# Expert tiles of the second half: results scattered to token order instead of gathered, with new order tables

## The chip, the cores and the metric

One core of one Trainium2 chip runs the kernel. The metric is the device time in microseconds (us) of one execution.

## What is computed

The input is x, 4 batches of 256 tokens of 128 numbers. Four layers are added to it one after the other, each on a layernormed x:

```
x = x + cross_attention_0(ln(x), ctx)       # 8 heads of 64, 512 context rows of 96
x = x + ffn_0(ln(x))                        # 128 -> 512 -> 128, fixed point, piecewise-linear gelu
x = x + cross_attention_1(ln(x), ctx)       # 16 heads of 8, then its own 128 -> 256 -> 128
x = x + moe(ln(x))                          # 8 experts, each token goes to its best two
# moe, per token t: sum over its two experts e of share[t, e] * (silu(t @ W1[e]) * (t @ W3[e])) @ W2[e]
```

## The kernel before

**One order for all engines.** `schedule()` makes one list of some 740 steps. A step is a name with indices, such as `("max", 1, 3, 5)`. Each engine walks the same list and executes its own part of each step, so the list sets the order of work within each of the five queues (PE, DVE, ACT, POOL, SP) and semaphores tie them together. The place of a step comes from tables: `PLACES` (per layer) and `SHIFTED` (per batch of a layer) give a place counted in attention heads, a pair meaning first place and distance. `REST` does this for the last part, in expert tiles.

**Attention** (places in heads): for each head, `max` computes scores and their row maxima on DVE (L879), `rows` transposes four heads' maxima on PE and copies them below the queries (L893), `sc` computes scores (L606) with an exponential on ACT (L1190), `av` multiplies with the values (L625, L638). Between them stand the steps of the feed-forward layer, of projections, loads of expert weights (`stage`) and their split in two fp16 parts on POOL (`split`).

**The mixture of experts** runs in two halves of 512 tokens (NT = 4 token tiles of 128, batches 0-1 and 2-3). For each half:
- `logits`, `route`, `shares`, `compare`, `rank` and `best` find the two best experts and their shares, all small DVE instructions. `rank` gives a mask, `count` counts tokens per expert on PE, and `place` (L1055 and on) gives each token two slots in a table of SLOTS = 15 tiles of 128 rows, sorted by expert, each expert's rows starting a new tile. `weights` puts the shares in the order of the two slots.
- `send` (POOL, L1360): eight indirect DMAs write 128 rows of 512 B each to the table `slots_in` in DRAM. `fetch` (SP, L1507) loads the table in four pieces, `gT` (L507, L1260, L1095) transposes and splits them.
- For each tile k (0 to 14 for half 0, 15 to 29 for half 1): `gu` (gate and up matmuls L781, silu L1268, product L1101), `hT` (transposes L792, L1274, L1105) and `dn` (down matmuls L800 and L803, ACT copy L1280, DVE sum L1112 into `y_sb`, four buffers, `k % 4`). `gu` of tile k has place k, `hT` k + 1.3, `dn` k + 2.6. SP's part of `dn` is `keep` (L1511): it stores the 64 KB result to the DRAM table `slots_out`, and DVE's next use of the buffer waits for that.
- `pick` (POOL, L1372): when all 15 stores of a half have landed, eight indirect DMAs gather the rows that belong to each token tile. `mix` (DVE, L1118 and L1119) adds two weighted rows to x, `store` (SP, L1515) writes the token tile out.

`pick 0` and `mix 0` run under tiles of half 1; `route`, `shares`, `best` and `weights` of half 1 stand behind tile 29, and `pick 1` and `mix 1` come last. In the profile names, `probs` holds y_sb and the gathered rows, `kS` and `kx` hold tokens and small arrays of this part, since buffers are used again.

Of the kernel before, what the change touches and what calls it, by code (L numbers as in the profile page):

```python
# [34 lines left out]
GROUPS = -(-SLOTS // 4)  # L35

# [3 lines left out]
    0: {"max": (1.86, 0.79), "sum": -0.41, "av": (3.3, 0.77), "f_ln": -2.84, "f_xn": -2.17, "f_xT": 4.05,  # L40
        "up0": (1.6, 0.1), "round": 7.85, "floor": 1.73, "nodes": -2.0, "slope": 6.04, "interp": 1.03,
# [3 lines left out]
        "zeros": -0.77, "wipe": -3.06, "init": (1.9, 2.63), "stack": 2.57, "rows": 3.42},  # L45
    1: {"max": (1.92, 0.8), "av": (1.04, 0.72), "f_ln": 1.67, "f_xn": 10.53, "f_xT": -6.55, "up0": (1.44, 0.53),
        "round": 2.56, "floor": 4.44, "nodes": 0.43, "slope": -4.29, "interp": 5.35, "ident": 12.62, "down0": 2.09,
        "q1_ln": 3.44, "q1_xn": 17.99, "q1_xT": 1.73, "q1": 12.78, "k1": 10.57, "bounce": 17.73, "sT": 2.58,
        "oT": (-3.52, 2.41), "aT": (3.56, 1.1), "y0": (3.34, 2.45), "oT1": (14.23, 0.44), "aT1": 4.66, "h1": 7.81,
        "y1": 15.69, "v1": 3.6, "stack": -2.4, "stage": (3.94, 1.45), "split": (1.35, 2.26), "consts": -5.47,  # L50
        "ex_ln": (4.78, 1.56), "ex_xn": (7.31, 1.05), "ex_xT": (5.75, 0.75), "logits": (9.25, 1.44),
        "route": 12.16, "shares": 10.26, "compare": 21.8, "rank": 21.45, "best": 18.11, "count": 18.16,
        "place": 17.23, "weights": 15.2, "send": 25.91, "fetch": 14.23, "gT": (19.54, 0.64), "rows": 3.88},
# [4 lines left out]
    (0, 'aT'): (3.66, 0.59), (0, 'av'): (-0.24, 0.54), (0, 'bounce'): 2.36, (0, 'down0'): 1.14, (0, 'f_ln'): -2.7,  # L58
    (0, 'f_xT'): 2.05, (0, 'f_xn'): 3.77, (0, 'floor'): -0.49, (0, 'ident'): 5.31, (0, 'init'): (1.06, 1.93),
    (0, 'interp'): 2.18, (0, 'k0'): (5.1, 0.6), (0, 'k1'): 2.26, (0, 'max'): (3.93, 0.56), (0, 'nodes'): 2.37,  # L60
    (0, 'oT'): (8.2, 1.03), (0, 'q0'): (6.54, 1.04), (0, 'q0_ln'): -1.54, (0, 'q0_xT'): 3.93, (0, 'q0_xn'): 2.69,
    (0, 'q1'): 4.85, (0, 'q1_ln'): 2.47, (0, 'q1_xT'): 8.92, (0, 'q1_xn'): 1.31, (0, 'round'): 3.34,
# [9 lines left out]
    (1, 'v0'): (7.68, 0.92), (1, 'v1'): 7.35, (1, 'wipe'): -3.17, (1, 'y0'): (6.57, 0.93), (1, 'zeros'): 6.25,
    (2, 'aT'): (5.59, 1.32), (2, 'av'): (-0.03, 0.96), (2, 'bounce'): 5.4, (2, 'down0'): 4.02, (2, 'f_ln'): -1.27,
    (2, 'f_xT'): 1.24, (2, 'f_xn'): 0.67, (2, 'floor'): 1.94, (2, 'ident'): 3.41, (2, 'init'): (-1.87, 2.14),
    (2, 'interp'): 3.32, (2, 'k0'): (2.17, 0.05), (2, 'k1'): 2.04, (2, 'max'): (1.54, 1.0), (2, 'nodes'): 2.29,
    (2, 'oT'): (5.07, 0.82), (2, 'q0'): (1.15, 1.29), (2, 'q0_ln'): -4.48, (2, 'q0_xT'): 1.23, (2, 'q0_xn'): -0.71,
    (2, 'q1'): 5.61, (2, 'q1_ln'): 4.16, (2, 'q1_xT'): 5.38, (2, 'q1_xn'): 4.63, (2, 'round'): 1.71,
    (2, 'rows'): 0.77, (2, 'sT'): 3.91, (2, 'slope'): 2.96, (2, 'stack'): 2.21, (2, 'sum'): 2.31,
    (2, 'up0'): (1.52, 0.14), (2, 'v0'): (3.77, 1.09), (2, 'v1'): 3.48, (2, 'wipe'): -0.07,
    (2, 'y0'): (6.04, 1.73), (2, 'zeros'): 8.64, (3, 'aT'): (5.76, 1.46), (3, 'av'): (-0.45, 0.96),  # L80
    (3, 'bounce'): 6.0, (3, 'down0'): 4.15, (3, 'f_ln'): -5.52, (3, 'f_xT'): 1.37, (3, 'f_xn'): 0.93,
    (3, 'floor'): 1.82, (3, 'ident'): 3.77, (3, 'init'): (-1.89, 2.22), (3, 'interp'): 3.51,
# [3 lines left out]
    (3, 'sT'): 3.7, (3, 'slope'): 3.25, (3, 'stack'): -6.1, (3, 'sum'): 1.34, (3, 'up0'): (1.58, 0.12),  # L86
    (3, 'v0'): (2.92, 0.59), (3, 'v1'): 5.21, (3, 'wipe'): 1.45, (3, 'y0'): (7.01, 0.57), (3, 'zeros'): 2.35,
    (4, 'aT'): (6.57, 2.0), (4, 'aT1'): 11.18, (4, 'av'): (-0.04, 1.0), (4, 'best'): 13.86, (4, 'bounce'): 12.33,
    (4, 'compare'): 14.92, (4, 'consts'): 12.05, (4, 'count'): 10.96, (4, 'down0'): 7.65,
    (4, 'ex_ln'): (9.16, 1.4), (4, 'ex_xT'): (9.35, 0.76), (4, 'ex_xn'): (8.67, 1.04), (4, 'f_ln'): 1.16,  # L90
# [1483 lines left out]
```

## Time and profile before

| | |
|---|---|
| median of 3 runs | 451.77 us (451.18 to 452.14) |
| the profiled execution's own time | 449.94 us |
| its span, first to last instruction | 447.8 us |
| mean granted TensorE clock | 0.941 |
| busy: PE / DVE / ACT / POOL | 381.1 / 323.1 / 241.6 / 195.3 us |
| HBM read / written | 15.11 / 7.86 MB |

Busy time is the time in which an engine executes; the rest of the span it waits. A row of the timeline gives the start, the busy time, the engine, the line of the kernel, the operation and output <- input; in brackets stands the idle time ahead of it and what ended it. The durations below are of the one profiled execution.

### The profile page before, as it was taken

What the parts mean: (1) busy time and instruction counts of PE and PEld (TensorE: products, weight loads), DVE (VectorE), ACT (ScalarE), POOL (GpSimd) and SP (SyncE); (2) the same over time, 40 slices, a digit from 0 to 9 for tenths busy, and PEclk for the clock granted to TensorE, in tenths of its full rate; (3) what the DMA queues carried; (4) which work ended last, traced back from release to release, by engine and by line L of the source; (5) the groups of instructions that cost most, each with busy time, mean ns of one, the idle gap of its engine ahead of it and who ended that gap; (6) DMA issues with size and microseconds to landing.
All of it is one profiled execution on the core that took longest, in us unless ns stands there. A gap on an engine that the chain in (4) does not pass through costs nothing.

```text
span 447.8 us, 8284 instructions
## 1 busy us (share of the span) xinstructions
PE 381.1 (85%) x2778; PEld 220.3 (49%) x2778; DVE 323.1 (72%) x668; ACT 241.6 (54%) x473; POOL 195.3 (44%) x252
## 2 busy tenths in 40 slices
PE   8667789999779868996997899998999789999930
PEld 3414444665356445553544355553454456777620
DVE  5765594667785799779888998789851685677752
ACT  3614455655734552467476666764676444665530
POOL 5135987726464493744418134660540015015014
PEclk9957999999899989998999699998999999999985
DMA  6572708008106106422043105420030002412112
GB/s 184 129 195 53 173 1 196 16 16 197 37 1 192 58 0 151 109 72 71 25 133 91 48 5 153 113 74 2 31 108 1 6 24 62 124 37 67 40 38 64
DMA packets 44766, 34.67 MB, mean 77 GB/s; under 512 B 5965, under 2 KB 41229, under 8 KB 44429
## 3 DMA queue, kind: packets, MB, share of 16 engines
q1 hardware_dynamic: 43701, 32.03, 27.6%
q0 software_dynamic: 1024, 2.10, 1.6%
q8 instruction: 24, 0.39, 0.4%
q14 instruction: 17, 0.14, 0.1%
HBM read 15.11 MB, written 7.86 MB: 51 GB/s over the span
## 4 chain that ended last, share of the span: by engine, by line
PE 51%; DVE 18%; issue 9%; ACT 8%; DMA 6%; POOL 4%; SPq 4%; POOLq 0%; DVEq 0%; ACTq 0%
PE p_sc L606 7%; PE p_misc L576 5%; PE p_o L625 5%; DVE mx L879 4%; PE p_misc L507 4%; PE p_misc L781 4%; PE p_sc L781 4%; PE p_o L638 4%; SPq L1434 4%; PE p_o L792 3%; PE p_misc L800 3%; PE p_misc L533 2%; DMA slots_in<-qx,kx 2%; DVE xn L849 2%; ACT probs L1190 2%
## 5 line engine op out<-in xcount | busy, mean ns | idle before, releaser
L879 DVE TENSOR_REDUCE mx<-p_misc 128x1 f32<-128x512 f32 x192 | 122.4, 683 | 26.3 <-PE p_misc L576 25.2
L1190 ACT ACTIVATE probs<-p_sc 128x512 f32<-128x512 f32 x192 | 104.5, 597 | 57.0 <-PE p_sc L606 56.4
L576 PE MATMUL p_misc<-kS,qS 96*128 96x512 f16 x128 | 40.9, 393 | 6.4 <-DVE mx L879 6.3
L606 PE MATMUL p_sc<-qS,kS 128*128 128x256 f16 x256 | 42.1, 283 | 3.2 <-ACT probs L1190 2.6
L1304 POOL TENSOR_SCALAR veps<-meanvar 128x2 f32<-128x2 f32 x16 | 3.8, 235 | 90.9 <-DVE meanvar L835 90.5
L1346 POOL TENSOR_TENSOR psums<-probs 128x256 f32<-128x256 f32 x32 | 24.7, 773 | 42.1 <-PE p_o L632 39.2
L638 PE MATMUL p_o<-probs,v 128*32 128x256 f32 x512 | 41.3, 401 | 0.4 <-issue 0.3
L625 PE MATMUL p_o<-probs,v 128*64 128x256 f32 x256 | 35.1, 395 | 4.0 <-ACT probs L1190 3.9
L1101 DVE TENSOR_TENSOR probs<-probs,p_sc 128x512 f32<-128x512 f32 x30 | 20.6, 686 | 24.4 <-ACT probs L1268 24.1
L1372 POOL DMA_INDIRECT probs<-slots_out,kx x16 | 15.2, 948 | 50.4 <-DMA slots_out<-probs 40.1
L606 PE MATMUL p_sc<-region 128*128 128x256 f16 x256 | 35.8, 286 | 0.9 <-DVE region L893 0.9
L1268 ACT ACTIVATE probs<-p_misc 128x512 f32<-128x512 f32 x30 | 17.9, 597 | 32.3 <-PE p_sc L781 32.3
L606 PEld LDWEIGHTS p_sc<-qS,kS 128*128 128x128 f16 x256 | 21.5, 100 | 25.9 <-issue 10.3
L606 PEld LDWEIGHTS p_sc<-region 128*128 128x128 f16 x256 | 24.8, 102 | 13.4 <-issue 5.2
L1360 POOL DMA_INDIRECT slots_in<-qx,kx x16 | 15.7, 984 | 33.3 <-issue 27.1
L1394 POOL TENSOR_TENSOR region<-v,region 128x512 f16<-128x512 f32 x24 | 28.8, 1200 | 1.9
L576 PE MATMUL p_misc<-region 128*128 128x512 f16 x64 | 21.8, 414 | 7.6 <-DVE cT L863 3.1
L1347 POOL TENSOR_TENSOR psums<-psums,probs 128x256 f32<-128x256 f32 x32 | 26.3, 821 | 2.5
L1348 POOL TENSOR_TENSOR psums<-psums,probs 128x256 f32<-128x256 f32 x32 | 25.5, 796 | 2.5
L625 PEld LDWEIGHTS p_o<-probs,v 128*64 128x64 f32 x256 | 15.8, 136 | 19.1 <-issue 9.4
L1393 POOL CAST region<-v 128x512 f16<-128x512 f32 x24 | 16.7, 695 | 15.8 <-DMA v<-in_L_ffn_W_dram 14.8
L1105 DVE TENSOR_TENSOR probs<-p_o,probs 128x512 f16<-128x512 f32 x30 | 20.5, 685 | 2.5 <-ACT probs L1274 2.5
(206 smaller groups left out, 741.5 us busy)
## 6 DMA issues: line engine op xcount, KB each, us to landing
region<-kx SPq DMA_DIRECT2D x24, 256.0 KB, 3.9
v<-in_L_ffn_W_dram SPq DMA_DIRECT2D x24, 256.0 KB, 2.8
region<-qx SPq DMA_DIRECT2D x24, 128.0 KB, 3.9
slots_in<-qS SPq DMA_DIRECT2D x2, 960.0 KB, 7.0
slots_out<-probs SPq DMA_DIRECT2D x30, 64.0 KB, 1.5
kS<-kS SPq DMA_DIRECT2D x1, 1664.0 KB
kS<-k_scratch SPq DMA_DIRECT2D x8, 192.0 KB
kS<-slots_in SPq DMA_DIRECT2D x6, 256.0 KB, 3.4
```

The source lines that it names most:

```text
L576: pe.matmul(ps, q[:, i * P:(i + 1) * P], k, start=True, stop=True).then_inc(full, 1)
L606: last = pe.matmul(p_sc[:, half, j * S:(j + 1) * S], k[:, kt * P:(kt + 1) * P], q, start=(i == 0), stop=(i == len(pairs) - 1))
L625: pe.matmul(p_o[64 * i:64 * i + 64, 0, m * S:(m + 1) * S], v0[:, b % 2, kt, h * DH0:(h + 1) * DH0], probs[:, h % 8, kt * S:(kt + 1) * S], ...
L638: last = pe.matmul(p_o[32 * j:32 * j + 32, n % 2, 0:S], v1[:, b % 2, c, h * VW:h * VW + 32], probs[:, h % 8, c * S:(c + 1) * S], start=(c ...
L781: last = pe.matmul(ps[:, k % 2, :], takenT[half][:, xs, at], w[:, bass.ds(chosen[k], 1), ws, :].rearrange("p e n -> p (e n)"), start=(i == ...
L879: dve.tensor_reduce(mx[:, b % 2, i, h:h + 1], ps, AX_X, ALU.max).then_inc(free, 1)
L1101: dve.tensor_tensor(hp[:, k % 2, :], sg[:, k % 2, :], p_sc[:, k % 2, :], ALU.mult).then_inc(hp_done, 1)
L1190: act.activation(probs[:, h % 8, half * 512:(half + 1) * 512], p_sc[:, half, :], ACT.Exp, scale=(DH0 if layer == 0 else DH1) ** -0.5).then ...
L1346: link(pool.tensor_tensor(psums[:, h % 4, :], tiles[0], tiles[1], ALU.add))
L1347: link(pool.tensor_tensor(psums[:, h % 4, :], psums[:, h % 4, :], tiles[2], ALU.add))
L1348: pool.tensor_tensor(psums[:, h % 4, :], psums[:, h % 4, :], tiles[3], ALU.add).then_inc(sums_set, 1)
L1394: pool.tensor_tensor(low, whole, high, ALU.subtract).then_inc(stage_free, 1)
```

## The change

In words: half 1's tile results no longer go to a slot table that is gathered once it is complete. Each row is scattered, as soon as its tile is done, to a DRAM table `token_rows` in which a token's two rows stand side by side, and SP then loads this table with plain DMAs.

- A row must know its destination. So the rows of half 1 get two more numbers (WIDE = 130, 520 B): twice the token's number plus 2, and the slot of the token's first row. They are written by DVE in `numbers` (new; one small matmul on PE and five DVE instructions, behind `aT1 3`) and in `place`, travel through send and fetch, and `dest` (new, four DVE instructions, between `dn 12` and `gu 15`) makes 15 columns of row numbers of them. Rows without a token get a row of their own at the table's end.
- `dn` of tiles 15 to 29 has a part on POOL, `to_tokens`, an indirect DMA, and none on SP. DVE waits for `y_sent` instead of `y_kept`.
- `pick` now has one step per token tile of half 0, each with two gathers, spread between tiles: pick 0 ahead of `hT 16` (so ahead of `dn 15`), pick 1 behind `dn 16`, pick 2 ahead of `dn 19`, pick 3 ahead of `dn 22`. Pick 1 of half 1 is gone; `back` (SP) waits for the last four scatters and loads four pieces of 128 KB, and `mix 1` waits for these.
- The four tables are rewritten. Of the mixture's steps: `best 0` and `weights 0` go from around `place 0` to the last batch (heads 1 and 12), `count 0` gets one max and one av step ahead of it, half 0's `gT` goes from head 11 and 12 to 14 and 15, `split 23` goes ahead of `send 0`, `fetch 1` from behind `dn 6` to behind `dn 8` (SP queue), and half 1's four late routing steps stay behind `dn 29`. In the attention parts most steps move by a few places; POOL's queue changes in 5 neighbouring exchanges there, SP's in 2.

```diff
-        (3.63, 'compare', 1), (3.68, 'rank', 1), (31.7, 'route', 1), (31.71, 'shares', 1), (31.72, 'best', 1), (31.73, 'weights', 1),
-        (4.79, 'count', 1), (4.84, 'place', 1), (5.44, 'send', 1), (8.85, 'fetch', 1), (13.62, 'gT', 1, 0),
-        (15.75, 'gT', 1, 1), (17.72, 'gT', 1, 2), (18.76, 'gT', 1, 3), (19.42, 'pick', 0), (20.61, 'mix', 0, 0),
-        (21.99, 'mix', 0, 1), (26.65, 'mix', 0, 2), (31.47, 'mix', 0, 3)]
+REST = [(0.16, 'oT1', 3, 0), (0.76, 'oT1', 3, 1), (1.09, 'aT1', 3), (1.16, 'numbers'), (1.77, 'h1', 3),
+        (1.82, 'y1', 3), (1.9, 'ln', 'ex', 3), (2.98, 'xn', 'ex', 3), (3.45, 'xT', 'ex', 3), (3.48, 'logits', 3),
+        (3.5, 'compare', 1), (3.92, 'rank', 1), (4.74, 'count', 1), (4.95, 'place', 1), (9.2, 'send', 1),
+        (11.34, 'fetch', 1), (13.99, 'gT', 1, 0), (14.99, 'dest'), (15.89, 'gT', 1, 1), (17.15, 'pick', 0),
+        (18.05, 'gT', 1, 2), (18.87, 'pick', 1), (20.69, 'gT', 1, 3), (21.4, 'pick', 2), (23.92, 'mix', 0, 0),
+        (24.54, 'pick', 3), (24.74, 'mix', 0, 1), (26.49, 'mix', 0, 2), (27.66, 'mix', 0, 3), (36.2, 'route', 1),
+        (38.8, 'shares', 1), (45.58, 'best', 1), (49.06, 'weights', 1)]
...
-    order += [("pick", 1)] + [("mix", 1, i) for i in range(NT)]
+    order += [("back",)] + [("mix", 1, i) for i in range(NT)]
...
+            def numbers():
+                pe.wait_ge(consts_set, 1)
+                ps, full = misc_take(pe, ("numbers",))
+                pe.matmul(ps[:, 0:SLOTS], before[:, :], all_ones[:, 0:SLOTS], start=True, stop=True).then_inc(full, 1)
...
+                if half == 1:
+                    dve.tensor_scalar(rows1[:, :, P + 1], slot[:, 0, :], 1.0, None, ALU.subtract)
...
+            def numbers():
+                dve.wait_ge(consts_set, 1)
+                ps, free = misc_wait(dve, ("numbers",))
+                link(dve.scalar_tensor_tensor(rows1[:, :, P], turn[:, 0:NT], float(P), ps[:, 0:NT], ALU.mult, ALU.add))
+                dve.tensor_scalar(rows1[:, :, P], rows1[:, :, P], 2.0, 2.0, ALU.mult, ALU.add)
+                dve.scalar_tensor_tensor(slot_number[:, :], turn[:, :], float(P), ps[:, 0:SLOTS], ALU.mult, ALU.add).then_inc(free, 1)
+                misc_done(dve, ("numbers",))
+                link(dve.tensor_scalar(own_row[:, :], slot_number[:, :], 2.0 * NT * P + 2, None, ALU.add))
+            def destinations():
+                for q in range(GROUPS):
+                    dve.wait_ge(ld_taken[q], 16 * 2)
+                link(dve.tensor_tensor(is_first[:, :], taken[:, :, P + 1], slot_number[:, :], ALU.is_equal))
+                link(dve.scalar_tensor_tensor(own_row[:, :], taken[:, :, P], 0.0, own_row[:, :], ALU.is_equal, ALU.mult))
+                link(dve.tensor_tensor(own_row[:, :], own_row[:, :], is_first[:, :], ALU.add))
+                dve.tensor_tensor(dest[:, :], taken[:, :, P], own_row[:, :], ALU.add).then_inc(dest_set, 1)
...
             def result(k):
-                if k >= 4:
+                if 4 <= k < SLOTS + 4:
                     dve.wait_ge(y_kept[k % 4], 16 * (k // 4))
+                elif k >= 4:
+                    dve.wait_ge(y_sent[k % 4], 16 * sent_of(k - 4))
...
+            def pick(i):
+                for s in range(4):
+                    pool.wait_ge(y_kept[s], 16 * ((SLOTS + 3 - s) // 4))
+                if i:
+                    pool.wait_ge(picked[i - 1], 16 * 2)
+                for s in range(2):
+                    pool.indirect_dma_start(picks[0][:, s, i, :], None, d_out,
+                                            bass.IndirectOffsetOnAxis(ap=slot_id[:, 0, s, i:i + 1], axis=0)).then_inc(picked[i], 16)
+            def to_tokens(k):
+                if k < SLOTS:
+                    return
+                misc_done(pool, ("ym", k))
+                if k == SLOTS:
+                    pool.wait_ge(dest_set, 1)
+                pool.indirect_dma_start(d_rows, bass.IndirectOffsetOnAxis(ap=dest[:, k - SLOTS:k - SLOTS + 1], axis=0),
+                                        y_sb[:, k % 4, :], None).then_inc(y_sent[k % 4], 16)
...
+            def back():
+                for k in range(2 * SLOTS - 4, 2 * SLOTS):
+                    sp.wait_ge(y_sent[k % 4], 16 * sent_of(k))
+                for i in range(NT):
+                    sp.dma_start(picks[1][:, :, i, :], d_rows[2 + 2 * P * i:2 + 2 * P * (i + 1), :].rearrange("(p s) n -> p s n", s=2)).then_inc(y_back[i], 16)
```

## Rows read from the trace of the kernel before

**Rows 1.** The page's busy time of each engine.
```profile
PE 381.1 (85%) x2778; PEld 220.3 (49%) x2778; DVE 323.1 (72%) x668; ACT 241.6 (54%) x473; POOL 195.3 (44%) x252
```

**Rows 2.** By stretch: length, busy PE, PEld, DVE, ACT, POOL; clock, DMA, GB/s.
```profile
60.00:300.00 240.00, 215.13 (x1602) 123.79 (x1600) 192.29 (x353) 140.65 (x267) 127.41 (x175) 0.96 0.31 81
300.00:320.00 20.00, 16.97 (x144) 6.72 (x144) 18.24 (x61) 11.45 (x25) 4.89 (x5) 0.91 0.07 21
369.00:430.00 61.00, 59.76 (x452) 41.69 (x449) 40.93 (x85) 34.16 (x76) 13.47 (x15) 1.00 0.22 64
```

**Rows 3.** The chain of waits, 429 to 448 us: start, duration, what.
```profile
430.62 2.43 DMA slots_out<-probs
...
433.09 0.70 issue
433.78 0.94 POOL probs L1372
...
442.53 2.57 DMA probs<-slots_out,kx
...
445.13 0.36 DVE x_sb L1118
...
445.51 0.35 DVE x_sb L1119
```

**Rows 4.** Timeline around the sends of both halves.
```profile
314.75 1.23 POOL L1360 DMA_INDIRECT slots_in<-qx,kx  x1 [12.93 <-issue]
...
365.81 0.17 DVE L1075 TENSOR_SCALAR kx<-kx 128x8 int32<-128x8 f32 x1
...
366.75 1.08 POOL L1360 DMA_INDIRECT slots_in<-qx,kx  x1 [11.16 <-issue]
```

**Rows 5.** The chain of waits at the last send of half 0.
```profile
327.55 2.95 DMA slots_in<-qx,kx
```

**Rows 6.** DMA issues: name, queue, operation, count, KB each, median us to landing.
```profile
q_scratch<-qx SPq DMA_DIRECT2D x4, 128.0 KB, 2.0
...
slots_in<-qx,kx POOLq DMA_INDIRECT x16, 2.2
probs<-slots_out,kx POOLq DMA_INDIRECT x16, 2.5
```

**Rows 7.** Timeline of POOL under half 1's tiles.
```profile
398.13 0.98 POOL L1372 DMA_INDIRECT probs<-slots_out,kx  x1 [20.23 <-DMA slots_out<-probs]
399.43 0.95 POOL L1372 DMA_INDIRECT probs<-slots_out,kx  x1 [0.30 <-issue]
403.56 0.95 POOL L1372 DMA_INDIRECT probs<-slots_out,kx  x1 [3.18 <-DMA probs<-slots_out,kx]
```

**Rows 8.** Fetch of half 0 by its tile: SP's issues, and landing times.
```profile
L1507 SPq DMA_DIRECT2D kS<-slots_in x4: 367/507/509, 330.5 to 332.0; - x4
...
DMA to landing us min/median/max: 2.8/3.7/4.1
```

**Rows 9.** Timeline of DVE in the tail.
```profile
434.37 0.17 DVE L1089 TENSOR_REDUCE kx<-kx 128x4 f32<-128x32 f32 x1
```

**Rows 10.** Timeline of DVE, tile 14's result.
```profile
395.43 0.28 DVE L1112 TENSOR_TENSOR probs<-p_misc,probs 128x128 f32<-128x128 f32 x1
```

**Rows 11.** Timeline of DVE at the first tiles.
```profile
352.72 0.42 DVE L910 TENSOR_TENSOR ytmp<-p_misc,f1b 128x256 f32<-128x256 f32 x1 [1.93 <-PE p_misc L730]
```

**Rows 12.** Timeline of DVE around best 0.
```profile
307.50 0.18 DVE L1049 SCALAR_TENSOR_TENSOR kx<-kx 128x32 f32<-128x32 f32 x1
```

**Rows 13.** What PE waited for, 300 to 345 us: total, times, longest.
```profile
PE p_misc L748 <- DVE kx L1043: 1.4, 1, 1.4
...
PE p_misc L507 <- DMA kS<-slots_in: 0.6, 2, 0.4
PE p_misc L576 <- DVE mx L879: 0.4, 1, 0.4
PE p_misc L507 <- DVE mx L879: 0.3, 1, 0.3
```

More of the change, by code:

```diff
@@ L35 @@
 GROUPS = -(-SLOTS // 4)
+WIDE = P + 2
 PLACES = {
-    0: {"max": (1.86, 0.79), "sum": -0.41, "av": (3.3, 0.77), "f_ln": -2.84, "f_xn": -2.17, "f_xT": 4.05,
-        "up0": (1.6, 0.1), "round": 7.85, "floor": 1.73, "nodes": -2.0, "slope": 6.04, "interp": 1.03,
[3 rows of a table removed]
[L45 to L53, printed above, removed]
@@ new lines @@
+    0: {"max": (-4.62, 1.13), "sum": 1.39, "av": (2.76, 1.36), "f_ln": 7.78, "f_xn": -8.15, "f_xT": -1.23,
+        "up0": (-2.85, 0.45), "round": 7.95, "floor": 6.62, "nodes": -8.25, "slope": 5.04, "interp": 7.44,
[3 rows of a table added]
+        "q0": (6.87, 0.66), "v1": 0.08, "zeros": -2.67, "wipe": -0.41, "init": (2.09, 2.98), "stack": 7.76,
+        "rows": 7.86},
+    1: {"max": (9.13, 1.48), "av": (-1.31, 0.11), "f_ln": 12.82, "f_xn": 17.1, "f_xT": -17.07, "up0": (6.69, 1.39),
+        "round": -18.46, "floor": 7.56, "nodes": -9.32, "slope": 5.47, "interp": -10.23, "ident": 10.47,
[3 rows of a table added]
+        "split": (6.74, 1.32), "consts": 0.86, "ex_ln": (0.38, 1.49), "ex_xn": (5.71, 1.53), "ex_xT": (9.95, 0.83),
+        "logits": (1.71, 2.04), "route": 12.72, "shares": 9.48, "compare": 22.49, "rank": 18.69, "best": 28.46,
+        "count": 24.36, "place": 10.34, "send": 30.88, "fetch": 3.74, "gT": (17.26, 1.85), "rows": 11.84,
+        "weights": 11.47},
@@ L54 @@
 }
 SHIFTED = {
[L58 to L62, printed above, removed]
@@ L72 @@
[L72 to L76, printed above, removed]
@@ L77 @@
[L77 to L82, printed above, removed]
[3 rows of a table removed]
@@ L86 @@
[L86 to L90, printed above, removed]
@@ new lines @@
+    (4, 'rank'): 17.2, (4, 'round'): 3.81, (4, 'route'): 3.68, (4, 'rows'): 4.05, (4, 'sT'): 3.63,
+    (4, 'send'): 20.25, (4, 'shares'): 17.27, (4, 'slope'): 6.05, (4, 'split'): (2.95, 1.2), (4, 'stack'): -0.22,
+    (4, 'stage'): (0.67, 1.64), (4, 'up0'): (3.08, 0.42), (4, 'v1'): 5.5, (4, 'weights'): 21.41,
+    (4, 'y0'): (7.8, 2.78), (4, 'y1'): -5.38, (5, 'aT'): (-6.56, 1.87), (5, 'aT1'): 5.47, (5, 'av'): (0.27, 1.06),
+    (5, 'best'): 19.69, (5, 'bounce'): 11.7, (5, 'compare'): 9.58, (5, 'consts'): 4.01, (5, 'count'): 12.43,
@@ new lines @@
+    (5, 'q1_xn'): 9.96, (5, 'rank'): 10.48, (5, 'round'): 2.45, (5, 'route'): 12.73, (5, 'rows'): 1.38,
+    (5, 'sT'): -5.5, (5, 'send'): 10.6, (5, 'shares'): 4.61, (5, 'slope'): 4.93, (5, 'split'): (0.78, 2.24),
+    (5, 'stack'): -8.2, (5, 'stage'): (-1.47, 2.13), (5, 'up0'): (2.12, 0.29), (5, 'v1'): 6.14,
+    (5, 'weights'): 13.36, (5, 'y0'): (14.39, 3.01), (5, 'y1'): 16.07, (6, 'aT'): (13.17, 1.5), (6, 'aT1'): 6.36,
+    (6, 'av'): (1.48, 0.73), (6, 'best'): 17.93, (6, 'bounce'): 4.86, (6, 'compare'): 12.04, (6, 'consts'): 2.19,
@@ new lines @@
+    (6, 'q1_xT'): 8.06, (6, 'q1_xn'): 13.98, (6, 'rank'): 13.35, (6, 'round'): -7.01, (6, 'route'): 11.83,
+    (6, 'rows'): 2.88, (6, 'sT'): -6.41, (6, 'send'): 21.24, (6, 'shares'): 13.9, (6, 'slope'): 2.81,
+    (6, 'split'): (0.76, 1.9), (6, 'stack'): -25.07, (6, 'stage'): (1.91, 2.25), (6, 'up0'): (-3.67, 0.22),
+    (6, 'v1'): 5.85, (6, 'weights'): 28.5, (6, 'y0'): (-1.71, 3.83), (6, 'y1'): 8.62, (7, 'aT'): (-18.57, 1.19),
+    (7, 'aT1'): 7.17, (7, 'av'): (0.38, 1.12), (7, 'best'): 29.72, (7, 'bounce'): 27.23, (7, 'compare'): 19.36,
@@ L547, in xt @@
                 pe.wait_ge(ln_xn, n + 1)
-                transposes(("xT", kind, b), [xn[:, n % 2, i, :] if kind != "ex" else xe[:, b * T + i, :] for i in range(T)])
+                transposes(("xT", kind, b), [xn[:, n % 2, i, :] if kind != "ex" else expert_rows(b * T + i) for i in range(T)])
             def queries0(b, i):
@@ L1124, in _ @@
                      "k1": keys1, "v1": values1, "q1": queries1, "oT1": heads_t1, "y1": add1, "logits": logits, "route": route, "shares": shares, "compare": compare, "rank": rank,
-                     "best": best, "place": place, "weights": weights, "gT": taken_t, "gu": product, "hT": low, "dn": result, "mix": mix}
+                     "best": best, "place": place, "weights": weights, "numbers": numbers, "dest": destinations, "gT": taken_t, "gu": product, "hT": low, "dn": result, "mix": mix}
             for kind, *at in order:
@@ L1355, in send @@
                     pool.wait_ge(zeroed, 32)
+                rows = xe[:, 0:NT, :] if half == 0 else rows1
                 for i in range(NT):
```

162 lines of the change are left out of this document (88 added, 74 removed), and 25 rows, old and new, of tables (PLACES, SHIFTED).

## The prediction

> **What bounds the kernel now.** I read the busy times first: TensorE (PE) is busy 85% of the span [rows 1]. The windows say where it isn't. From 369 to 430 us, the body of the expert tiles, PE is busy 59.76 of 61 us [rows 2]; behind it the kernel lasts 17.8 us more. The chain of waits through this tail shows why [rows 3]: the last tile's result is written at 430.6 and its store to DRAM lands 2.43 us later, POOL needs 0.70 us to wake, then eight indirect gathers of 0.94 us follow, (442.53 - 433.78)/7 = 1.25 us apart, the last lands 2.57 us after its issue begins, and two VectorE (DVE) instructions and a store of 447.8 - 445.86 = 1.94 us end the kernel. Eight gathers of 1.25 us, all behind the last tile, are what the tail consists of. Elsewhere PE sets the pace with short stalls: 3.0 us in 300 to 320, where DVE is busy 18.24 of 20 us, and 24.9 us in 60 to 300 [rows 2].
>
> **The tail.** The change takes the eight gathers, the store before them and their waits out of the tail, and puts in: one scatter by POOL, a wait of SP, four direct loads of 128 KB, and the same four pairs of DVE instructions and four stores. Step by step from 430.60:
> - POOL's wake behind DVE: its first send begins at 366.75, DVE's index write ended at 365.81 + 0.17 = 365.98, so 0.8 us [rows 4]. The scatter of tile 29 begins at 431.4. The scatter of tile 28 is no obstacle: that tile's result is 1.4 us earlier and an issue holds POOL 1.25 us.
> - The trace has no scatter of tile results, but the sends are the same operation (128 rows of 512 B to DRAM). From the start of the last send to SP's first dependent issue is 2.95 us [rows 5]: 434.35. Ends: 2.2, the median landing of a send, and 403.56 - 399.43 = 4.13, the slowest indirect transfer shown [rows 6, 7]. I take 2.95, since there too SP is the one who waits.
> - SP's four loads: the nearest rows are the fetch's pieces of 256 KB, with 2.8/3.7/4.1 us; a 128 KB transfer lands in 2.0 us at best [rows 6, 8]. I take 2.8 for the first: 437.15. SP issues one in 0.5 us [rows 8], less than the 0.77 us a pair of mix instructions takes, so behind the first DVE sets the pace.
> - Four mix pairs, 445.51 - 445.13 + 0.35 = 0.73 each and 0.04 between: 3.0 us [rows 3]: 440.2. The last store, 1.94: the end is at 442.1 instead of 447.8, **-5.7 us**.
> The ends: 431.4 + 2.2 + 2.0 + 3.0 + 1.94 = 440.6 (-7.2), and 431.4 + 4.13 + 4.1 + 3.0 + 1.94 = 444.6 (-3.2). The routing arithmetic of half 1 (route, shares, best, weights) stays behind the last tile on DVE. It ends at 434.5 [rows 9], hidden by the scatter and the loads up to 437.15; without that cover it would cost its 4 us.
>
> The Trainium skill ("DMA: Bandwidth & Descriptors", section "Anatomy of one DMA — SWDGE (gpsimd) path") speaks against this exchange: most of a DMA's fixed cost of some 2 us is the wait for the write receipt, heaviest where the target is HBM, and the scatter writes to DRAM where the gather wrote to SBUF. Here the rows order them the other way: sends to DRAM land in 2.2 us, gathers into SBUF in 2.5 [rows 6]. By the rule the scatter would take at least the gather's 2.57 us, which lies inside the 2.95 taken.
>
> **The second half's tiles.** POOL now has 15 scatters and 8 gathers between tile 14's result at 395.7 [rows 10] and 430.6. At 1.25 us each these are 28.8 of 34.9 us. Before, the gathers alone were there, and each pair waited for the one before (3.18 us idle ahead of 403.56) [rows 7]. In the new order scatters of tiles 15 and 16 stand behind pick 0, 17 and 18 behind pick 1, 19 to 21 behind pick 2 and the rest behind pick 3. I walk this queue with a result every 34.9/15 = 2.33 us. Pick 0 starts at 398.1 and pick 1 at 403.6, as before; scatter 17, ready at 402.7, starts behind pick 1 at 403.6 + 2.5 = 406.1 and lands 2.95 later at 409.1. DVE wants its buffer for tile 21, at 412.0. Scatters 15 and 16 fit between the picks, and later ones wait less, so I price the new wait for y_sent at 0; without those 2.9 us of margin each us late would be a us of the kernel. Stores of half 1 leave SP's queue; nothing waits behind them.
>
> DVE gets nine small instructions of 0.17 to 0.2 us. Five (numbers, with a tiny matmul) stand ahead of tile 0's low part, in a stretch where DVE idles 1.93 us before 352.72 [rows 11]: 0.2 us, ends 0 and 1.0. Four (dest) come at about 390, where DVE is busy 40.9 of 61 us [rows 2]: 0.1, ends 0 and 0.9. Together **+0.3**. The 520-byte rows load sends and fetch by 1.6%. The fetch of half 1 is moved behind the stores of tiles 7 and 8 on SP, to about 381 us; gT needs it near 386.5, and the landing takes 2.8 to 4.1: 0.
>
> **The order.** Two moves have a price that the rows show. `best` (five instructions of 0.2 us from 307.50 on [rows 12]) and `weights` (five of the same kind) leave the DVE-bound stretch before and behind `place` for the time of the last batch, and `count` gets a maxima and a values step of PE ahead of it. The stalls there are 1.4 us of count, 0.4 and 0.3 us of maxima and rows [rows 13]. I take **-1.5**, ends 0 and -2.1. Half 0's gT goes from behind head 11 to behind head 14 of the last batch, so PE's 0.6 us of waiting for the fetch goes, **-0.6**, ends 0 and -0.6 [rows 13]. Everything else in the tables shifts steps by a few places among 24.9 us of stalls [rows 2]. Queues of SP and POOL barely change, `rows` mostly stands farther behind its maxima (good for PE, bad for the scores that need it). I find no sum: 0, ends -3 and +3.
>
> **Sum.** -5.7 + 0.3 - 1.5 - 0.6 = -7.5 us on the profiled execution, span 447.8 to 440.3. That execution took 449.94, 2.1 more than its span; the median shown is 451.77, 1.83 above it. So 451.77 - 7.5 = **444.3 us**.
>
> **Rivals.**
> - A, slower: POOL becomes the bound of the second half. An indirect issue beside a busy DVE costs more than 1.25 us, results wait for their y_sb buffer, and PE behind them. 23 issues fill the 34.9 us at 1.52 us each, and eat the whole gain at 42.4/23 = 1.84 us. At twice the issue time (2 x 0.95 + 0.3 = 2.2 us): 50.6 - 34.9 = +15.7, so 460. For: one send took 1.23 instead of 0.96 [rows 4]. Against: the gathers at 398 and 403 ran at 0.98 and 0.95 beside a working DVE [rows 7]. Chance 0.05. The Trainium skill ("SBUF — State Buffer", section "A bandwidth-pool intuition that's wrong") has this mechanism as a port lock: an indirect DMA of 0.62 us took 3.1 beside a DVE copy. By that, 2.5 us more per issue, half 1 would cost +51 us; the gathers' rows don't show it, and the tiles' DVE instructions read PSUM.
> - B, less gain: scatter and loads at their slow ends, the tail gives 3.2 only: 446.8. For: gathers took up to 4.13. Chance 0.14.
> - C, the order decides: if the other moves take a third of the 24.9 us, 444.3 - 8 = 436 (0.09); if they cost as much, 452 (0.06, half of it within 0.2%).
> - D, the change doesn't do what it says: the token rows aren't ready behind tile 15, because dest waits for all four pieces of the fetch on DVE. It takes effect from a fetch landing after 390, 5 us later than I expect, and each us later delays tile 15 as much; at 10 us late, 449. Chance 0.03.
> The forecast itself: 0.63.
>
> **Numbers.** This kernel's measurement tells about 0.2%, 0.9 us, from no change. Tail ends of +2.5 and -1.5, order ends of 3 us, and -0.6 of the priced stretches give the range: 444.3 - 5.1 = 439.2 to 444.3 + 5.5 = 449.8. It holds the forecast, B and D, and leaves out A and C, 0.2 together. Faster 0.89 (forecast, B, C's first half, D), same 0.03, slower 0.08 (A and half of C's other half).
>
> **What would show it.** In the tail: no gather behind the last result, one scatter starting 0.8 us behind it, SP's first load 3 us later, four mix pairs without waits between them, the end 11.5 us behind the last result instead of 17.2. In half 1: PE busy as before, POOL at about 80% with DVE never waiting for y_sent. In 300 to 320: PE idle under 2 us. A DVE wait for a POOL transfer in 400 to 430, or a last result later than 429 to 430.5, would prove me wrong, and a last result before 425 would say that the order tables matter more than the tail.

## The result and the profile after

The changed kernel takes 448.67 us (median of 19 runs, 444.16 to 455.7), the kernel before 451.77 in the same comparison. The ratio is 0.9906, with a 95% interval of 0.9886 to 0.9926: faster by 0.9%. It leaves out the five slowest executions of the kernel after, over 1.5% above its fastest; with all 19 the medians stand at 0.993. Forecast were 444.3 us and a range of 439.2 to 449.8. The direction and the range held, but only 3.1 of the 7.5 us came by the medians, 4.2 by the ratio.

The profiled execution after took 447.96 us, span 446.1, against 449.94 and 447.8 before. Split at four events of the two timelines (my subtraction, us from the span's start):

| | before | after | difference |
|---|---|---|---|
| silu of tile 0 begins | 346.2 | 344.1 | -2.1 |
| silu of tile 15, first tile of half 1, begins | 390.8 | 391.4 | +2.7 within this stretch |
| silu of tile 29 begins | 425.6 | 431.6 | +5.4 within this stretch |
| result of tile 29 done | 430.6 | 436.6 | 0 |
| end | 447.8 | 446.1 | -7.7 in the tail |

The tail first, in the chain of waits of the kernel after (start, duration, what); it answers to [rows 3]:

```profile
436.89 2.26 DMA token_rows<-probs,kx
...
439.23 2.16 DMA probs<-token_rows
...
441.48 0.36 DVE x_sb L1172
...
443.82 0.35 DVE x_sb L1172
```

No gather is left. The scatter of tile 29 begins 0.3 us behind the result, lands in 2.26, SP's first load takes 2.16, and the eight mix instructions run without long waits. From result to end it is 9.5 us, where before it was 17.2.

The windows after (length, busy PE, PEld, DVE, ACT, POOL; clock, DMA, GB/s), the same stretches as in [rows 2], and the tiles of half 1 from silu of tile 15 to that of tile 29:

```profile
60.00:300.00 240.00, 215.37 (x1612) 124.15 (x1614) 193.97 (x353) 142.16 (x270) 125.51 (x173) 0.97 0.32 80
300.00:320.00 20.00, 16.60 (x151) 6.78 (x144) 19.04 (x56) 11.36 (x25) 8.86 (x9) 1.00 0.13 38
369.00:430.00 61.00, 56.72 (x411) 37.94 (x411) 38.45 (x82) 30.92 (x70) 24.16 (x25) 1.00 0.21 61
391.40:431.60 40.20, 36.60 (x265) 24.33 (x264) 25.98 (x55) 19.97 (x46) 18.56 (x20) 1.00 0.15 43
```

And the last of these stretches in the kernel before:

```profile
390.80:425.60 34.80, 34.80 (x266) 24.56 (x265) 24.55 (x51) 20.39 (x46) 7.62 (x8) 1.00 0.17 48
```

Before, PE was never idle in half 1. After, the same matmuls take 40.2 us at the same granted clock of 1.00 (2.4 GHz). The timeline of one place shows who is late (start, busy, engine, line, what, idle ahead and what ended it); L808 makes silu's input, L819 the turn, L1324 silu, L1330 the high part of `hT`, L1336 the result's low half:

```profile
401.38 1.00 POOL L1437 DMA_INDIRECT token_rows<-probs,kx  x1 [0.30 <-issue]
...
401.68 0.60 PE L819 MATMUL p_o<-ident,probs 128*128 128x128 f32 x4
...
402.56 0.39 PE L830 MATMUL p_misc<-region,probs 128*128 x4
402.69 0.97 POOL L1437 DMA_INDIRECT token_rows<-probs,kx  x1 [0.30 <-issue]
...
403.10 0.60 ACT L1324 ACTIVATE probs<-p_misc 128x512 f32<-128x512 f32 x1 [1.96 <-PE p_sc L808]
...
404.00 0.98 POOL L1427 DMA_INDIRECT probs<-slots_out,kx  x1 [0.34 <-issue]
...
405.26 0.59 ACT L1330 CAST probs<-p_o 128x512 f16<-128x512 f32 x1 [1.57 <-PE p_o L819]
405.28 0.96 POOL L1427 DMA_INDIRECT probs<-slots_out,kx  x1 [0.30 <-issue]
405.88 0.69 DVE L1152 TENSOR_TENSOR probs<-p_o,probs 128x512 f16<-128x512 f32 x1 [1.47 <-ACT probs L1330]
...
407.44 0.27 ACT L1336 COPY probs<-p_misc 128x128 f32<-128x128 f32 x1 [1.59 <-remote]
```

ScalarE (ACT) is late. Its order in half 1 is silu of one tile, high part of the tile before, result of the tile before that. PE's matmuls for the silu at 403.10 begin at 401.04 and take 0.81, so the input is there at 401.85 and the start is 1.25 us late, where 0.04 is usual. The high part at 405.26 belongs to the turn that ended at 401.68 + 0.60 = 402.28: 3.0 us late. The result at 407.44 belongs to L830, which ended at 402.95: 4.5 us late. The three instructions start 2.2 us apart with their inputs long there (the names behind the arrows are of later groups of PE). ScalarE's instructions themselves last no longer than before, DVE and PE start promptly behind it, and POOL's issues last 0.96 to 1.00 us. This happens in three places, 398.8 to 406.2, 410.0 to 414.8 and 418.4 to 423.2, and in these POOL issues six, four and four indirect transfers with 0.30 to 0.34 us between them. What waits DVE had from 391 to 437 us, half 1 and the two results behind it (engine, line, for whom: us in total, times, longest):

```profile
DVE probs L1148 <- ACT probs L1324: 6.6, 13, 0.9
DVE probs L1148 <- issue: 3.6, 2, 2.0
DVE probs L1161 <- ACT probs L1336: 2.1, 3, 1.2
DVE probs L1152 <- ACT probs L1330: 2.0, 2, 1.5
```

There is no wait for a scatter among them.

The +2.7 us ahead of tile 15 go with a fall of the granted clock. This stretch of the first tiles, in the kernel before, after, and in a second profiled execution of the kernel after, in this order:

```profile
345.00:357.00 12.00, 9.15 (x57) 5.67 (x55) 6.54 (x18) 6.11 (x12) 0.93 (x2) 1.00 0.00 0
```
```profile
345.00:357.00 12.00, 9.50 (x44) 6.19 (x45) 6.60 (x22) 3.79 (x8) 0.93 (x2) 0.72 0.00 0
```
```profile
345.00:357.00 12.00, 9.41 (x62) 6.36 (x60) 6.92 (x22) 5.77 (x11) 0.93 (x2) 1.00 0.00 0
```

At 0.72 the engine was at its lower level, 1.2 GHz, for over half of the stretch (0.28 of the 0.5 between the levels): three matmuls of a gate took 1.49 us from 351.70 on, against 0.81 in the kernel before. PE had idled 1.61 us ahead of 346.5, but it idled as long ahead of 348.6 in the kernel before and ahead of 349.0 in the second execution, and no fall followed. Why it fell in one and not in the others isn't shown. In the second execution silu of tile 0 to silu of tile 15 takes 44.4 us, in the kernel before 44.6.

### The profile page after: what moved, and what is told of

It reads as the page before. It is cut to its first block, busy times and chain, and to the rows that moved or that the text cites. A ratio compares the mean times of both kernels' runs of the same rounds, so it can differ in the third digit from the quotient of the medians.

```text
span 446.1 us, 8303 instructions
## 1 busy us (share of the span) xinstructions
PE 383.8 (86%) x2779; PEld 221.4 (50%) x2779; DVE 328.2 (74%) x677; ACT 240.8 (54%) x473; POOL 201.1 (45%) x259
## 4 chain that ended last, share of the span: by engine, by line
PE 51%; DVE 23%; POOL 6%; issue 6%; ACT 5%; SPq 4%; DMA 4%; another core or an unknown queue 0%; POOLq 0%; DVEq 0%; ACTq 0%
PE p_sc L627 7%; DVE mx L906 6%; PE p_misc L597 5%; PE p_o L659 5%; PE p_o L646 4%; PE p_misc L808 4%; SPq L1499 4%; PE p_sc L808 4%; PE p_misc L528 4%; PE p_o L819 3%; PE p_misc L827 3%; PE p_misc L554 2%; PE p_misc L701 2%; POOL kS L1366 2%; DMA region<-qx 2%
## 5 line engine op out<-in xcount | busy, mean ns | idle before, releaser
L627 PE MATMUL p_sc<-qS,kS 128*128 128x256 f16 x256 | 40.6, 276 | 1.7 <-ACT probs L1246 1.1
L646 PE MATMUL p_o<-probs,v 128*64 128x256 f32 x256 | 36.2, 405 | 3.4 <-ACT probs L1246 3.4
L627 PE MATMUL p_sc<-region 128*128 128x256 f16 x256 | 34.4, 279 | 2.2 <-DVE region L920 2.2
L1324 ACT ACTIVATE probs<-p_misc 128x512 f32<-128x512 f32 x30 | 17.9, 598 | 31.9 <-PE p_sc L808 29.0
L1459 POOL TENSOR_TENSOR region<-v,region 128x512 f16<-128x512 f32 x24 | 28.7, 1196 | 1.9
L597 PE MATMUL p_misc<-region 128*128 128x512 f16 x64 | 20.7, 398 | 6.1 <-DVE kx L895 3.3
L1458 POOL CAST region<-v 128x512 f16<-128x512 f32 x24 | 15.5, 646 | 14.0 <-DMA v<-in_L_ffn_W_dram 13.1
L1437 POOL DMA_INDIRECT token_rows<-probs,kx x15 | 14.6, 975 | 14.5 <-DVE probs L1161 12.9
L827 PE MATMUL p_misc<-region,probs 128*128 x120 | 18.5, 274 | 3.0 <-issue 2.1
```

Source lines behind the costliest of these rows:

```text
L597: pe.matmul(ps, q[:, i * P:(i + 1) * P], k, start=True, stop=True).then_inc(full, 1)
L627: last = pe.matmul(p_sc[:, half, j * S:(j + 1) * S], k[:, kt * P:(kt + 1) * P], q, start=(i == 0), stop=(i == len(pairs) - 1))
L646: pe.matmul(p_o[64 * i:64 * i + 64, 0, m * S:(m + 1) * S], v0[:, b % 2, kt, h * DH0:(h + 1) * DH0], probs[:, h % 8, kt * S:(kt + 1) * S], ...
L827: pe.matmul(ps[:, 0:2 * P], hh[:, k % 2, 0, f * P:(f + 1) * P], w, start=(f == 0), stop=False)
L1459: pool.tensor_tensor(low, whole, high, ALU.subtract).then_inc(stage_free, 1)
```

## The experiments

Theory: dense runs of indirect issues on POOL make ScalarE answer late in half 1. Rivals: the scatters alone, the order of the steps, the number of indirect transfers, or gathers and scatters in flight together. All times are medians; "half 1" is silu of tile 15 to silu of tile 29 in the profiled execution, 34.8 us before. Twelve kernels ran in four groups, each beside the kernel before on the same chip (452.12, 452.33, 454.14 and 452.26 us), so ratios compare better than times. Half 1 is read from one execution each, and that one isn't always typical: in after_again, two_in_flight, spread and singles_two_in_flight it stood +0.8, -2.2, -2.0 and +0.8 us from the kernel's median.

| kernel | us | ratio to before (95%) | half 1, us |
|---|---|---|---|
| after, first / again | 448.67 / 449.5 | 0.9906 / 0.993 (0.9902 to 0.9958) | 40.2 / 43.1 |
| no_gathers | 441.25 | 0.9764 (0.9734 to 0.9794) | 34.9 |
| plain_stores | 442.21 | 0.9765 (0.9747 to 0.9782) | 34.9 |
| before_new_order | 449.32 | 0.9939 (0.9926 to 0.9952) | 34.8 |
| after_old_order | 449.57 | 0.994 (0.9915 to 0.9966) | 41.8 |
| apart | 450.42 | 0.9963 (0.9941 to 0.9985) | 38.8 |
| two_in_flight | 446.0 | 0.9852 (0.9824 to 0.988) | 35.8 |
| spread | 446.81 | 0.9886 (0.9868 to 0.9903) | 40.1 |
| every_other | 449.67 | 0.9908 (0.9875 to 0.9942) | 39.5 |
| gathers_in_a_row | 457.58 | 1.0079 (1.0051 to 1.0106) | 40.6 |
| gathers_in_fours | 452.19 | 1.0008 (0.9985 to 1.0032) | 36.9 |
| singles_two_in_flight | 446.14 | 0.9857 (0.9813 to 0.9902) | 38.8 |

**Which part costs.** no_gathers leaves out half 0's eight gathers (their tokens get no expert rows); plain_stores leaves out the token order of half 1 (SP stores its rows plainly).

no_gathers, in `pick` and in DVE's `mix`:

```diff
-                for s in range(2):
-                    pool.indirect_dma_start(picks[0][:, s, i, :], None, d_out,
-                                            bass.IndirectOffsetOnAxis(ap=slot_id[:, 0, s, i:i + 1], axis=0)).then_inc(picked[i], 16)
+                return
...
-                if half == 0:
-                    dve.wait_ge(picked[i], 16 * 2)
-                else:
+                if half == 1:
```

plain_stores, in `to_tokens` on POOL and in SP's store step of tiles 15 to 29:

```diff
-                pool.indirect_dma_start(d_rows, bass.IndirectOffsetOnAxis(ap=dest[:, k - SLOTS:k - SLOTS + 1], axis=0),
-                                        y_sb[:, k % 4, :], None).then_inc(y_sent[k % 4], 16)
+                return
...
+                    at = 2 + (k - SLOTS) * P
+                    sp.dma_start(d_rows[at:at + P, :], y_sb[:, k % 4, :]).then_inc(y_sent[k % 4], 16)
```

> The changed kernel without the eight gathers of half 0 (their rows are left out; the mixes of half 0 read what the buffer holds). Theory 1: ScalarE answers late when gathers and scatters follow each other on POOL without a pause (the trace of the changed kernel lost 5.2 us between tiles 16 and 23, in the three places where POOL issues 3 to 6 in a row). Then the tiles come every 2.4 to 2.5 us again and the time is about 443.5 us, with less spread. Rival 1: the scatters alone do it; then the losses stay and the time is 448 to 449. Rival 2: the order of PE's and DVE's steps does it; then it is 448 to 449 too.

> The changed kernel with half 1's results stored by plain DMAs of SP instead of scattered by POOL (the token order is left out); the gathers of half 0 stay where they are. Theory 1 and rival 1 both expect the loss of 5.2 us under the tiles to go: about 443 us. Rival 2 (the order of steps, not the transfers): 448 to 449.

With either kind alone half 1 is back at its length before: 15 scatters alone cost nothing, 8 gathers alone, in pairs with a wait between them, cost nothing. Both times came out lower than expected, no_gathers by 2.3 us.

**The order.** before_new_order is the kernel before with the new PLACES and SHIFTED tables, after_old_order the kernel after with the old ones; REST and the code stay.

> The kernel before with the new tables for the attention parts and the token steps, its own order of the expert tiles. By the two traces the first expert tile came 2.1 us earlier with the new tables (silu of tile 0 at 344.1 against 346.2). Theory: the tables are worth 2 us, 449.8 us. Rival: the clock's stretches at half speed fell differently and the tables are worth nothing, 451.8; or the new order leaves PE idle ahead of the tiles more often and it is 453.

> The changed kernel with the old tables for the attention parts and the token steps. Theory: 2 us slower than the changed kernel, 450.7, with the same spread of the runs (444 to 456), since that comes from the expert tiles. Rival: the spread and part of the loss come from the new tables; then 446 with a small spread.

The tables give 2.8 us to the kernel before (452.12 to 449.32) and 0.5 to 1.5 us to the kernel after (0.994 against 0.993 and 0.9906, the intervals overlap), where some 2 us were expected of both. Half 1 loses with either order, so the order is not its cause.

**How the issues lie.** apart keeps gathers and scatters from being in flight together; two_in_flight lets at most two be on their way; spread issues gathers singly, one behind each of eight scatters; after_again repeats the kernel.

apart, in `pick` (and its steps at 17.15, 20.7, 24.7, 28.7 in REST):

```diff
-                if i:
-                    pool.wait_ge(picked[i - 1], 16 * 2)
+                for k in tiles_ahead[i]:
+                    pool.wait_ge(y_sent[k % 4], 16 * sent_of(k))
...
+                pool.wait_ge(picked[i], 16 * 2)
```

two_in_flight, called ahead of each gather and each scatter:

```diff
+            def room_for(sem_, count):
+                if len(flying) >= 2:
+                    pool.wait_ge(*flying[-2])
+                flying.append((sem_, count))
```

spread, one gather for each step:

```diff
+REST = [(17.65, 'pick', 0), (18.65, 'pick', 1), (19.65, 'pick', 2), (20.65, 'pick', 3), (21.65, 'pick', 4), (22.65, 'pick', 5), (23.65, 'pick', 6), (24.65, 'pick', 7),
```

> As after, but a gather of half 0 and a scatter of half 1 are never in flight together: POOL waits for the scatters ahead to land before it issues a pair of gathers, and for the pair before it goes on; the pairs stand further apart (one about every fourth tile). Nothing is left out. Theory (gathers and scatters issued into each other without a pause make ScalarE answer late in half 1, 5.3 us in all): the stretch from silu of slot 15 to the last is back near 35 to 36 us against 40.2, and the time is 443 to 444.5. Rival 'number of indirect DMAs': the count of 23 on POOL is what matters, not how they lie; then it stays at 448 to 449. Rival 'waits': POOL's new waits hold the scatters up and the four result buffers fill, DVE waits; then it is 450 or more.

> As after, with the same places of all steps, but POOL waits before each gather and each scatter until at most one other of them is still in flight. Nothing is left out. Theory (unbroken runs of issues): the issues come at least 1.2 us apart as the landing takes 2.2 to 2.5 us, so the runs of 1.3 us pitch are nearly as dense as before; a small part of the 5.3 us returns, 447 to 448.5. Rival 'more than two in flight at once is the cost': all of it returns, 443 to 444.5.

> As after, but the eight gathers go singly, one behind each scatter of tiles 16 to 23, where after has them in four pairs; each mix follows its pair. Nothing is left out. Theory (unbroken runs of issues on POOL, whatever their kind): POOL issues two per tile of 2.4 us, which is its full pitch of 1.25 us, so the run is unbroken for eight tiles and the loss is as in after or more, 449 to 451. Rival 'a gather right behind another gather, with scatters queued behind both, is what delays ScalarE': no such pair is left, 443.5 to 445.

> The changed kernel once more, unedited, on the chip of the three others. Its time: 448.5, between 446 and 451. If the fall of the granted clock at 347 to 354 us in the first profile was chance, this one shows none there and the gap between silu of tiles 1 and 2 is 7.0 us as before, against 9.6; if it belongs to the change it is there again. Silu of slot 15 to the last takes 40 us again if the loss in half 1 belongs to the kernel and not to that execution.

apart's time is that of the rival of waits, 450 or more, but DVE waited for no scatter. Nothing of a gather and a scatter overlaps, and yet half 1 still takes 38.8 us, 4.0 more than 34.8. No wait of DVE for a transfer stands in it; the one for the last gathers, 2.15 us ahead of 434.96, comes behind the last result. The timeline of POOL and ScalarE in it:

```profile
401.22 1.00 POOL L1442 DMA_INDIRECT token_rows<-probs,kx  x1 [2.96 <-DMA probs<-slots_out,kx]
402.53 0.97 POOL L1442 DMA_INDIRECT token_rows<-probs,kx  x1 [0.31 <-issue]
403.81 0.96 POOL L1442 DMA_INDIRECT token_rows<-probs,kx  x1 [0.30 <-issue]
405.07 0.96 POOL L1442 DMA_INDIRECT token_rows<-probs,kx  x1 [0.30 <-DMA token_rows<-probs,kx]
```
```profile
402.10 0.58 ACT L1330 CAST probs<-p_o 128x512 f16<-128x512 f32 x1
...
404.77 0.60 ACT L1324 ACTIVATE probs<-p_misc 128x512 f32<-128x512 f32 x1 [1.26 <-PE p_sc L808]
406.91 0.59 ACT L1330 CAST probs<-p_o 128x512 f16<-128x512 f32 x1 [1.54 <-remote]
```

Its waits pile the scatters up, four of them then leave at 1.3 us pitch. ScalarE is 0.5 us late at 404.77, under the third (input at 403.48 + 0.81 = 404.29), and 2.2 late at 406.91 (turn over at 404.73). So gathers and scatters in flight together are not needed for the loss. Its tail also grew, to 14.1 us, as the last two gathers and the waits held the last scatters up. two_in_flight returns 4.4 of the 5.4 us in its profiled execution, more than the theory gave it, pays 1 us in the tail (10.5 from result to end), and is the fastest kernel of the study that leaves nothing out. By the ratios it still stands 4.0 us behind no_gathers, 1 of them in the tail, so typical executions seem to keep more of the loss than this one shows. spread has half 1 as in after, as expected of a dense run, though no gather stands right behind another gather there, so that rival fails. Its time was better than expected, 446.81; its profiled execution has no fall of the clock at 345 to 357. after_again has none there either, so the fall doesn't come with every execution of the changed kernel (of the variants' profiled executions every_other's has it too, 0.72 again), but it has a still longer half 1.

**Runs of one kind, and dose.** gathers_in_a_row and gathers_in_fours are before_new_order, where nothing scatters in half 1, with the waits between pairs of gathers removed, or kept only in the middle. every_other is spread with gathers behind every other scatter.

gathers_in_a_row:

```diff
-                    if half == 0 and i:
-                        pool.wait_ge(picked[i - 1], 16 * 2)
```

gathers_in_fours:

```diff
-                    if half == 0 and i:
+                    if half == 0 and i == 2:
```

every_other:

```diff
+REST = [(17.15, 'pick', 0), (17.16, 'pick', 1), (18.65, 'pick', 2), (20.65, 'pick', 3), (22.65, 'pick', 4), (24.65, 'pick', 5), (26.65, 'pick', 6), (28.65, 'pick', 7),
```

> The kernel before with the changed kernel's order of steps in both tables (before_new_order), and its eight gathers of half 0 issued without the waits between the pairs: one unbroken run of eight at 1.3 us, some 10 us long, in the middle of half 1's tiles, with no scatter anywhere near. Nothing is left out. Theory (unbroken runs, whatever their kind): ScalarE answers late in that stretch from the third or fourth issue on; silu of slot 15 to the last takes 36.5 to 38 us against 34.8 and the time rises from 449.3 to 451 to 452.5. Rival (it needs scatters among the gathers): 34.8 us and 449.3.

> gathers_in_a_row with one wait put back, in the middle: two unbroken runs of four gathers with a pause of some 1.5 us between them, no scatters near. Nothing is left out. Theory with a start at the third or fourth issue: two stalls of 0.5 to 1.5 us in place of three of over 2, silu of slot 15 to the last 35.5 to 37.5 us (34.8 in pairs, 40.6 in one run of eight), time some 2 us above before_new_order: ratio to before 0.996 to 1.002. Rival (every issue beyond the second of a run costs the same, some 1 us): 38.5 us.

> As spread, but the single gathers stand behind every other scatter only (two ahead of the first scatter, then one behind the scatters of tiles 16, 18, 20, 22, 24 and 26), so that POOL never issues more than three indirect transfers without a pause of a microsecond. Nothing is left out, no wait is added. Theory (unbroken runs of four and more issues on POOL make ScalarE answer late, whatever their kind): silu of slot 15 to the last takes 35 to 35.8 us (34.9 where no gathers are issued, 35.8 with two in flight, 40 in spread and after) and the time is 441.5 to 443.5, under both kernels. Rival 'gathers and scatters in flight together': they still are in eight places, so the stretch stays at 38 us or more and the time at 446 or more.

gathers_in_a_row settles the theory. One run of eight gathers, 400.17 to 409.9, nothing else changed, and half 1 goes from 34.8 to 40.6 us, more than expected. The timeline of it, PE's rows first, then ScalarE's (L1271, L1277, L1283 are silu, high part, result here):

```profile
403.38 0.60 PE L795 MATMUL p_o<-ident,probs 128*128 128x128 f32 x4
...
404.25 0.39 PE L806 MATMUL p_misc<-region,probs 128*128 x4
```
```profile
402.28 0.48 ACT L1263 CAST probs<-p_misc 128x384 f16<-128x384 f32 x1
405.94 0.60 ACT L1271 ACTIVATE probs<-p_misc 128x512 f32<-128x512 f32 x1 [3.17 <-remote]
408.83 0.58 ACT L1277 CAST probs<-p_o 128x512 f16<-128x512 f32 x1 [2.30 <-PE p_o L795]
411.76 0.27 ACT L1283 COPY probs<-p_misc 128x128 f32<-128x128 f32 x1 [2.34 <-remote]
```

Three instructions in 9 us, 2.9 us apart. Silu's input was there at 403.54 (2.4 us late), the high part belongs to the turn that ended at 403.98 (4.8 late), the result to L806, over at 404.64 (7.1 late). Behind the run the pace is 2.4 us again. The time rose more than expected too, some 6 us (ratio 1.0079 against 0.9939) where 1.7 to 3.2 stood in the expectation. In fours the loss is 2.1 us, in pairs none, so runs of two, four and eight cost 0, 2.1 and 5.8 us for the same eight gathers, read from one execution each, and their number is not what costs. In the last the granted clock of this stretch stood at 0.96, behind idle times of PE of up to 2.3 us. every_other missed: its first five issues (399.13 to 404.26) stood in one run, because pick 0 and pick 1 came right ahead of two scatters, and once tiles were late the results came in pairs and made new runs. Runs of three delayed ScalarE there as well: the results at 425.85 and 431.11 start 0.9 and 1.3 us behind their inputs, each behind three issues with 0.30 us between them.

**Both remedies.** singles_two_in_flight has every_other's places and two_in_flight's waits.

> Both remedies together: the single gathers of every_other (behind every other scatter) and the waits of two_in_flight (at most two indirect transfers of half 1's stage on their way at once). Nothing is left out. Theory (a run of issues on POOL costs from its third or fourth issue on): no run is longer than two, silu of slot 15 to the last takes 35 to 35.6 us and the time is 444.5 to 446 on a chip where before takes 452 (ratio 0.984 to 0.986, as two_in_flight or a little better). Rival (pauses of 0.4 to 0.8 us are too short, what counts is how many issues fall in some 10 us): 37 us or more, ratio over 0.99.

The ratio met the theory (0.9857), half 1 the rival (38.8 us). The waits allow three issues in a row where the earlier transfer has landed in time; six issues between 418.34 and 425.38 had pauses of at most 0.74 us, and ScalarE fell behind there. It had fallen behind from 409.94 on as well, where no more than two issues in a row had 0.30 us between them and the pauses around them were 0.53 to 0.75 us: so at most two on their way isn't enough by itself. It is no better than two_in_flight. How long a pause must be to count stays open: in two_in_flight no more than two issues in a row stand 0.30 to 0.34 us apart, and the other pauses are 0.44 to 1.2 us:

```profile
402.83 0.97 POOL L1445 DMA_INDIRECT token_rows<-probs,kx  x1 [0.45 <-issue]
404.44 0.97 POOL L1434 DMA_INDIRECT probs<-slots_out,kx  x1 [0.64 <-issue]
405.72 0.96 POOL L1434 DMA_INDIRECT probs<-slots_out,kx  x1 [0.30 <-issue]
407.86 1.00 POOL L1445 DMA_INDIRECT token_rows<-probs,kx  x1 [1.18 <-issue]
```

## Why the prediction was half right

**The tail: right, and under-sized.** Priced at -5.7, measured -7.7, outside the better end of -7.2. Three terms were too dear. The 0.8 us of POOL's wake became 0.3, since POOL had issued tile 28's scatter until just before. The scatter and SP's start took 2.3, where I had 2.95 from [rows 5], a row of POOL issues in pairs. The first load took 2.2 where I had 2.8 from the 256 KB pieces of [rows 8]; the 2.0 of [rows 6] was the nearer row, since its size is the same. The four mix pairs took 2.7, where I had 3.0; the last store, 1.9, was as priced. The rule of the Trainium skill on write receipts ("DMA: Bandwidth & Descriptors", section "Anatomy of one DMA — SWDGE (gpsimd) path") carried no weight here: the scatter into DRAM landed in 2.26 us, sooner than the gathers' 2.5.

**The routing's cover: nearly gone.** I had DVE done with it at 434.5 and the data at 437.15. It ended at 440.58 and the data came at 441.4. It cost nothing, by 0.8 us.

**The order: right in sum, unclear in place.** Priced at -2.1; the tables alone gave -2.8. But PE's idle time in 300 to 320 did not fall under 2 us, it is 3.4, so the stalls that I named (1.4 us of count, 0.7 of maxima and rows) gave way to others, 1.9 and 1.2 us of waiting for row maxima. The -2.1 at silu of tile 0 is partly the clock: it was at 0.91 in 300 to 320 before and at 1.00 after, and after_again, with 0.91 there, begins this silu at 346.6.

**The step that failed** is the walk of POOL's queue, "so I price the new wait for y_sent at 0". What it says of y_sent is true, DVE never waited for it. The error is that the walk looked at waits alone and took POOL's load, 28.8 of 34.9 us, as free so long as its queue drained. Half 1 lost 5.4 us (8.3 in after_again) because dense issues delay ScalarE. I named DVE waiting for a scatter in 400 to 430, or a last result later than 430.5, as what would prove me wrong. The second came, at 436.6, without the first. The time still fell into the range, and that is in part luck: the range had no term for the loss of half 1, nor for the fall of the clock. The tail's extra gain of 2.0 us took a part of it up, and the 5.5 us kept on the slow side for the order and the tail held the rest. That slow side also left out that the 2.1 us priced for the order might not come.

**Rival A** had the right place and the wrong mechanism. Each issue should have grown beside a busy DVE; they stayed at 0.96 to 1.00 us, so its price of 15.7 us never arose, nor was there a sign of the port lock that stood behind it. The figure of the Trainium skill that the prediction gives there ("SBUF — State Buffer", section "A bandwidth-pool intuition that's wrong") is for a DMA issued from GpSimd, and the page doesn't say that it was an indirect one. B, slow transfers, was wrong in sign. C did not come either way. Nor did D: dest was written and scatter 15 left at 401.38, held only by pick 0 ahead of it.

Summed in the profiled execution: -2.1 + 2.7 + 5.4 - 7.7 = -1.7, which is 446.1 - 447.8. With the loss of half 1 taken out, as in no_gathers and plain_stores, the ratio is 0.9765, better than the forecast's 444.3/451.77 = 0.983; both leave out work, so this bounds what a remedy can give.

## What to carry to other kernels

Count POOL's indirect DMAs not only against POOL's own time. Where ScalarE stands in the critical loop, lay out how many of them follow each other without a pause: pairs with a wait behind them were free here, two runs of four cost 2.1 us and a run of eight 5.8. A cap of two on their way, by waits on POOL, gave 446.0 us, ratio 0.9852, and is the version to take, though it doesn't remove the loss. And a throttle that looks idle, as the wait between pairs of gathers in the kernel before, may be what keeps the loop whole: without it that kernel's ratio went from 0.9939 to 1.0079, some 6 us.
